# Additions of the mixing and of the residual on VectorE, the mixing bias by ScalarE inside the bank, and a new order of the steps

## The reference, cut to what matters

```python
# layer 0
Mn = conv(Wn, bn, inorm(x_c)); Mm = conv(Wm, bm, inorm(x_s))
A  = softmax(einsum('bct,bcs->bts', Mn, Mm))
x  = conv(Wo, bo, einsum('bcs,bts->bct', conv(Wl, bl, x_s), A)) + x_c
# layer 1
xa  = ln(x); sx = shift(xa) - xa
xxx = tanh((xa + sx * maa_x) @ maa_w1).reshape(b, l, 5, 32)
xxx = einsum('blfd,fde->blfe', xxx, maa_w2)            # low rank, five mixes
xk, xw, xv, xr, xg = xa + sx * (maa_stack + xxx)       # the five mixed inputs
w = exp(-exp(time_decay + tanh(xw @ td_w1) @ td_w2))
r, k, v, g = xr @ Wr.T, xk @ Wk.T, xv @ Wv.T, silu(xg @ Wg.T)
s = k_t v_t^T + w_t * s                                # scan over 128 tokens
out_t = r_t (u * k_t v_t^T + s)
x1 = x + (groupnorm(out) * g) @ Wo.T
y  = x1 + sigmoid(xr2 @ Wfr.T) * (square(relu(xk2 @ Wfk.T)) @ Wfv.T)
```

## Time and profile before

| | |
|---|---|
| median of three executions | 1966.55 us |
| the profiled execution | 1968.96 us |
| its span, first to last instruction | 1967.2 us |
| TensorE (PE) busy | 1824.0 us, 93% |
| VectorE (DVE) busy | 1843.6 us, 94% |
| ScalarE (ACT) busy | 1037.8 us, 53% |
| GpSimd (POOL) busy | 1064.5 us, 54% |
| mean granted TensorE clock | 0.978 |

### The profile page before, as it was taken

The page is one execution under the profiler, slowest core; times in us unless marked ns, Lnnn a source line. Parts: engine busy times, 40 slices in busy tenths (PEclk is TensorE's granted clock), DMA queues, the critical chain, the costliest instruction groups (busy, mean ns, idle before and its releaser), DMA issues.

```text
span 1967.2 us, 34835 instructions
## 1 busy us (share of the span) xinstructions
PE 1824.0 (93%) x12548; PEld 1276.5 (65%) x12548; DVE 1843.6 (94%) x2564; ACT 1037.8 (53%) x2177; POOL 1064.5 (54%) x822
## 2 busy tenths in 40 slices
PE   5779999999999999999999999999999999999865
PEld 3556666676666767666677666666766666676633
DVE  3599999999999999999999999999999999999981
ACT  3434556555555655554565555565555556555322
POOL 1245565556656555565555556655565565555531
PEclk8899999999999999999999999999999999999877
DMA  5233333333333333333333333333333233333320
GB/s 231 76 98 90 81 100 103 98 104 97 96 84 101 98 105 101 94 95 86 98 98 109 96 98 84 95 103 98 103 102 97 81 101 102 99 93 86 91 67 11
DMA packets 86201, 189.31 MB, mean 96 GB/s; under 512 B 18800, under 2 KB 35312, under 8 KB 85008
## 3 DMA queue, kind: packets, MB, share of 16 engines
q1 hardware_dynamic: 64528, 170.32, 31.4%
q10 hardware_dynamic: 21504, 16.78, 2.8%
HBM read 161.91 MB, written 16.78 MB: 91 GB/s over the span
## 4 chain that ended last, share of the span: by engine, by line
PE 58%; DVE 17%; POOL 15%; issue 9%; ACT 1%; POOLq 0%; DMA 0%; DVEq 0%; SPq 0%; ACTq 0%
PE bank L957 24%; POOL hrs L400 8%; PE bank L1004 6%; PE bank L964 5%; PE bank L1080 5%; DVE S L605 5%; PE bank L969 5%; DVE xf L570 3%; DVE S L614 3%; DVE S L596 2%; POOL xf L428 2%; POOL rku L434 2%; POOL S L444 2%; PE bank L1036 2%; PE bank L975 2%
## 5 line engine op out<-in xcount | busy, mean ns | idle before, releaser
L605 DVE TENSOR_TENSOR_SCAN S<-wrep,S 128x1024 f32<-128x1024 f32 x256 | 592.3, 2314 | 1.6 <-POOL S L444 1.1
L444 POOL COPY S<-s 128x8 f32<-128x8 f32 x256 | 173.4, 692 | 484.0 <-PE bank L1080 473.1
L428 POOL TENSOR_TENSOR xf<-xf,xa 128x512 f32<-128x512 f32 x160 | 337.4, 2116 | 124.1 <-DVE xf L570 124.1
L614 DVE TENSOR_TENSOR S<-S,rT 128x1024 f32<-128x1024 f32 x256 | 339.4, 1326 | 0.2
L596 DVE TENSOR_TENSOR S<-vrep,kT 128x1016 f32<-128x1016 f32 x256 | 319.1, 1247 | 3.5 <-PE bank L1080 3.4
L398 POOL TENSOR_SCALAR rstd<-mv 128x1 f32<-128x1 f32 (+1 forms) x96 | 128.6, 1340 | 236.8 <-DVE mv L510 143.6
L570 DVE SCALAR_TENSOR_TENSOR xf<-bank,par,sx 128x128 f32<-128x128 f32 x640 | 178.8, 341 | 13.3 <-PE bank L1036 9.5
L1080 PE MATMUL bank<-S,slide 128*32 128x256 f32 x2048 | 171.4, 397 | 9.5 <-DVE S L614 9.5
L400 POOL TENSOR_TENSOR hrs<-hrs,mhalf 128x32 f32<-128x32 f32 x32 | 175.5, 5485 | 2.7
L957 PEld LDWEIGHTS bank<-xf,Wk 128*128 128x128 f32 x1024 | 118.4, 194 | 50.0 <-issue 50.0
L957 PE MATMUL bank<-xf,Wk 128*128 128x128 f32 x1024 | 123.5, 280 | 25.9 <-DVE xf L570 25.9
(11 more groups left out here) (129 smaller groups left out, 3650.7 us busy)
## 6 DMA issues: line engine op xcount, KB each, us to landing
vrep<-v_dram SPq DMA_DIRECT2D x256, 512.0 KB
xc<-x_c SPq DMA_DIRECT2D x32, 256.0 KB, 4.0
xs<-x_s SPq DMA_DIRECT2D x32, 256.0 KB, 4.9
v_dram<-vT ACTq DMA_DIRECT2D x32, 256.0 KB, 2.6
xres<-xin SPq DMA_DIRECT2D x32, 256.0 KB, 6.5
out<-rr ACTq DMA_DIRECT2D x32, 256.0 KB, 4.4
Wv<-big_w SPq DMA_DIRECT2D x1, 1024.0 KB, 7.1
Wk<-big_w SPq DMA_DIRECT2D x1, 1024.0 KB, 9.1
```

The lines of the kernel that those rows point to most:

```text
L428: po.tensor_tensor(xf[:, b, :, :], xf[:, b, :, :], xa[:, :, 1:P + 1], ALU.add).then_inc(pool_mid.sem, 1)
L444: po.tensor_copy(S[:, u % 2, :, 0], s0[:, p, k:k + UJ]).then_inc(pool_wkv.sem, 1)
L605: ve_.tensor_tensor_scan(s, wrep[:, u % C, :, :].rearrange("p j t -> p (j t)"), s, 0.0, ALU.mult, ALU.add).then_inc(dve_wkv.sem, 1)
L614: ve_.tensor_tensor(s, s, rT[:, p, u % C, :].unsqueeze(1).broadcast_to([P, UJ, P]), ALU.mult).then_inc(dve_wkv.sem, 1)
```

## The change

It has four parts.

1. `mid_mix`: ScalarE first adds `maa_stack` in the bank itself (`mid_bias`, four instructions of 128 x 128 per mix). VectorE then multiplies the bank by `sx` in one instruction of 128 x 512 and adds `xa` in a second one; GpSimd's `mid_add` is gone.
2. `fin_y`: VectorE adds `x1` itself; GpSimd's `fin_out` is gone.
3. `mid_W1`: `xx` is now the stationary operand, four products of 160 columns with tokens on the partitions. ScalarE takes tanh into a new tile `txn`, TensorE transposes it back in two pieces (`mid_Wt`), ScalarE copies these to `tx` and `txg` (`mid_txt`).
4. A new order of all lists. `mid_Tx` and `mid_xa` move from the step of `b1` to the end of that of `b0`; the projections of r and g move from `b2` to `b1`; `tail_C`, `tail_To`, `tail_o`, `tail_sq` from `b3` to `b2`; `tail_Tx2`, `tail_FK`, `fin_FR`, `fin_kr` from `b4` to `b3`. The element's last piece, `fin_FV` to `fin_store`, stays in `b4`. The rings of banks and the counts follow.

```diff
 FRONT_JOBS = [(j, int(lag)) for j, lag in (x.split(":") for x in (
-    "Rp:2 G:2 V:0 Tx:1 Mn:0 Mm:0 W1:1 Mv:1 Mw:1 S0:0 S1:0 S2:0 Mk:1 Mr:1 S3:0 Vp:1 D1:1 Kp:1 Mg:1 "
-    "T0:0 T1:0 T2:0 T3:0 D2:1 E2:1 O:0").split())]
+    "Mn:0 Mm:0 S0:0 S1:0 S2:0 W1:1 Wt:1 V:0 S3:0 Mv:1 Mw:1 Mk:1 Mr:1 Vp:1 D1:1 Kp:1 Mg:1 D2:1 "
+    "E2:1 T0:0 T1:0 T2:0 T3:0 O:0 Rp:1 G:1 Tx:0").split())]
 BACK_JOBS = [(j, int(lag)) for j, lag in (x.split(":") for x in (
-    "Tx2:4 FK:4 C:3 FR:4 FV:4 Tg:3 Wo:3").split())]
+    "FV:4 Tg:3 Wo:3 Tx2:3 FK:3 C:2 FR:3").split())]
...
-            def mid_add(n, m, p, i):
-
-                f, b = ORDER[i], i % 3
-                eng.wait_ge(dve_mid.sem, dve_mid.count(f"m{f}", n))
-                po.tensor_tensor(xf[:, b, :, :], xf[:, b, :, :], xa[:, :, 1:P + 1],
-                                 ALU.add).then_inc(pool_mid.sem, 1)
...
-            def fin_out(n, m, p):
-                eng.wait_ge(dve_fin.sem, dve_fin.count("y", n))
-                po.tensor_tensor(rr[:, :], rr[:, :], x1[:, :], ALU.add).then_inc(pool_fin.sem, 1)
...
-                eng.wait_ge(pe_mid.sem, pe_mid.count(f"M{f}", n))
+                eng.wait_ge(act_mix.sem, act_mix.count(f"b{f}", n))
                 eng.wait_ge(pe_mid.sem, pe_mid.count(last_use, n if i >= 3 else n - 1))
-                ps = bank_of(f"M{f}")
-                for c in range(C):
-                    last = ve_.scalar_tensor_tensor(xf[:, b, c, :], ps[:, c * P:(c + 1) * P],
-                                                    col("maa_stack", c, MIX.index(f)), sx[:, c, :], ALU.add, ALU.mult)
-                last.then_inc(dve_mid.sem, 1)
+                ve_.tensor_tensor(xf[:, b, :, :], by_chunk(bank_of(f"M{f}")[:, :]), sx[:, :, :],
+                                  ALU.mult).then_inc(dve_mid.sem, 1)
+                eng.wait_ge(dve_mid.sem, dve_mid.count(f"m{f}", n))
+                ve_.tensor_tensor(xf[:, b, :, :], xf[:, b, :, :], xa[:, :, 1:P + 1],
+                                  ALU.add).then_inc(dve_mid.sem, 1)
...
                 ve_.tensor_tensor(rr[:, :], bank_of("FV")[:, :], rr[:, :], ALU.mult).then_inc(dve_fin.sem, 1)
+                eng.wait_ge(dve_fin.sem, dve_fin.count("y", n))
+                ve_.tensor_tensor(rr[:, :], rr[:, :], x1[:, :], ALU.add).then_inc(dve_fin.sem, 1)
...
+            def mid_bias(n, m, p, f):
+
+                eng.wait_ge(pe_mid.sem, pe_mid.count(f"M{f}", n))
+                for c in range(C):
+                    ps = bank_of(f"M{f}")[:, c * P:(c + 1) * P]
+                    last = sc.activation(ps, ps, ACT.Identity, bias=col("maa_stack", c, MIX.index(f)))
+                last.then_inc(act_mix.sem, 1)
...
-                ps = bank_of("W1")
-                for c in range(C):
-                    pe.matmul(ps[:, 0:P], w1[:, c, 0:P], xx[:, c, :], start=(c == 0), stop=(c == C - 1))
-                for c in range(C):
-                    last = pe.matmul(ps[0:DM, P:2 * P], w1[:, c, P:P + DM], xx[:, c, :],
+                for c in range(C):
+                    last = pe.matmul(bank_of("W1")[:, 0:5 * DM], xx[:, c, :], w1[:, c, :],
                                      start=(c == 0), stop=(c == C - 1))
                 last.then_inc(pe_mid.sem, 1)
+
+            def mid_Wt(n, m, p):
+
+                eng.wait_ge(act_mid.sem, act_mid.count("tn", n))
+                eng.wait_ge(*bank_free("Wt", n))
+                pe.transpose(bank_of("Wt")[:, 0:P], txn[:, 0:P], ident[:, :])
+                pe.transpose(bank_of("Wt")[0:DM, P:2 * P], txn[:, P:P + DM], ident[:, :]).then_inc(pe_mid.sem, 1)
```

More of the change, by code:

```diff
@@ L142, in build @@
         txg = sb("txg", [DM, P])
+        txn = sb("txn", [P, 5 * DM])
         xf = sb("xf", [P, 3, C, P])
@@ L415, in mid_xa0 @@
                 v0 = held(eng, regs[0], 16 * (m + 1))
-                v1 = held(eng, regs[1], dve_mid.count("xx", n - 1))
-                v2 = held(eng, regs[2], pool_mid.count("fg", n - 1))
+                v1 = held(eng, regs[1], dve_mid.count("fg", n - 1))
                 eng.wait_ge(pool_const, CONSTS)
@@ L647, in tail_x1 @@
                 eng.wait_ge(xres_copied[p], 16 * (m + 1))
-                eng.wait_ge(pool_fin.sem, pool_fin.count("out", n - 1))
+                eng.wait_ge(dve_fin.sem, dve_fin.count("out", n - 1))
                 ve_.tensor_tensor(x1[:, :], bank_of("Wo")[:, :], xres[:, p, :], ALU.add).then_inc(dve_tail.sem, 1)
@@ L733, in step @@
+                if b2: tail_o(*b2)
                 if b1: wkv_scan(*b1, 0)
+                if b0: att_rstd1(*b0)
             run(step)
@@ L894, in fin_store @@
             def fin_store(n, m, p):
-                eng.wait_ge(pool_fin.sem, pool_fin.count("out", n))
+                eng.wait_ge(dve_fin.sem, dve_fin.count("out", n))
                 dst = out[n] if isinstance(n, int) else out[bass.ds(n, 1)].rearrange("o p f -> (o p) f")
@@ L1000, in att_O @@
             def att_O(n, m, p):
+                eng.wait_ge(act_att.sem, act_att.count("v", n))
                 eng.wait_ge(*bank_free("O", n))
```

236 lines of the change are left out of this document (118 added, 118 removed).

## The result

The changed kernel takes 2006.8 us in the median (2003.4 to 2008.5) against 1967.5 us for the kernel before on the same chip: a ratio of 1.0195, interval 1.0181 to 1.0208, 39 us slower. The prediction was 1961 us with a range of 1943 to 1990; it was wrong in sign, and the time lies outside its range.

What follows compares the result with a forecast made beforehand. VectorE, busy 297.4 of 300 us, was taken as the bound. 1968.96 us profiled, +0.3 (added work against contention), +3 (att_rstd1), -9.3 (ends) gave 1963.0; less 2.4 for the median, about 1961 us, range 1943 to 1990.

Steps and rivals of the forecast that it cites:

- Mixing +40 us: VectorE's mixes, as a product and a chained addition, take 1.29 us each, +0.25 a mix, +40 us in all.
- residual +22.7 us: VectorE's residual: the product loses its 0.11 us overlap and a 0.60 us addition follows, +22.7 us over 32 elements.
- A chained start costs 0.11 us: On VectorE a dependent instruction starts 0.03 us behind its predecessor's end, where unchained neighbours overlap by 0.08 us.
- Rival F: A chained start on VectorE costs nothing, 21 us less than the forecast: 1940 us; chance 0.02.
- Contention: 72.4 us go, 10 come back: GpSimd's large instructions hold up VectorE's by 72.4 us; most goes with the additions, 10 us stays for the rest.
- Rival C: GpSimd's product r x k meets outer1, which starts 1.07 us late in each element: +24 us, 1985 us; chance 0.12.
- The wait at `att_rstd1`, 3 us: Behind scan0, VectorE may wait some 0.5 us for GpSimd's power, 17 us in 32 elements; 3 us was taken.
- Bias covered, cost nothing: ScalarE's bias delays each mix by 1.5 us, hidden as mixes stand later; cost nothing, uncovered 0.5 us.
- Low-rank part, nothing counted, -0.4 to +0.5 us per element: TensorE's low-rank work shrinks by 0.4 us but adds a round trip through ScalarE; nothing was counted.
- TensorE fits with some tenths in hand: Between unit 5's read and the next read0, TensorE needs 16.5 to 17 us, ScalarE 0.6, against VectorE's 17.6.
- Rival B: VectorE starts to wait, att_xin for O or read0 for rT; at 0.6 us a step 1980 us; chance 0.27.
- The ends: Fill and drain: the end, from last read to variance, saves 9.3 us; the start counts 0, within 3 either way.

Runs made afterwards that it cites:

- e7_unchained: e1_rk_late with another VectorE instruction between the product and the addition of each mix and of the residual; 1966.2 us, ratio 0.9984.
- e4_old_order: The kernel before with only VectorE's additions and ScalarE's bias from the change, old order and old low-rank part; 2091.4 us, ratio 1.0627.
- e1_rk_late: The changed kernel with GpSimd's product r x k moved behind the initial columns of unit 3, as before; 1979.6 us, ratio 1.0060.
- e9_more_unchained: The kernel of e7_unchained with six more VectorE pairs drawn apart and the addition of xr behind scan 6; 1979.1 us, ratio 1.0054.
- e5_lowrank_ring: The changed kernel with the old low-rank products, keeping the transposes' slot in the ring of banks; 2026.0 us, ratio 1.0289.
- e8_start: e1_rk_late with the low-rank product W1 and the first mix taken earlier, in step 1 only; 1979.0 us, ratio 1.0055.

## Why the prediction was wrong, point by point

- **VectorE sets the pace.** Right in the middle; the step is its list plus small waits.
- **Mixing +40 us, residual +22.7 us.** Nearly right. By the table above the mixes cost 1.43 us a step, 46 in all (0.71 and 0.61 for a pair, where 1.29 was worked out), the residual 0.73, 23 in all.
- **A chained start costs 0.11 us.** Right, by the pairs of e7_unchained. Rival F falls; the rule of the Trainium skill behind it, "VectorE: DVE Perf Modes", section "The DRAIN you can't avoid", does not hold here (0.60 against 0.71 us).
- **Contention: 72.4 us go, 10 come back.** This is the step that failed: what is left of the contention was sized at 10 us and measured 31.7. That the additions were the cause is right for some 61 of the 72.4 us (e4_old_order); the other 11 were already the product r x k, which stays, so the 10 taken are about what it had cost in its old place. In the new place it costs 31.7 us by the mean of L596, near the upper end of the bounds (0 to 34). Moving it away in e1_rk_late gave 27 back, some 3 of them by the clock, while it still cost 0.14 us a step there. By the table the net gain is 1.16 us a step, where 2.26 - 0.31 = 1.95 was in the sum. Two choices stood behind the 10. The place: "comes while VectorE does read0 and outer1" was right, and both of these have two inputs in SBUF, so there was no cover at all. The row: the copy at 1076.87, where waiting GpSimd let two of VectorE's instructions pass, was taken as the likely course; but the product doesn't find read 0 running, it starts 0.09 us ahead of it, behind the small nmr, and then holds it. Rival C was this mechanism with the right price and, but for element 12, the wrong victim (read 0, not outer 1). In element 12 the product did find read 0 running, and it did not let outer 1 pass as the copy had done: it went as rival C had it. Why the copy waited for two instructions and the product for one is open. The Trainium skill, "GPSIMD Engine Reference", section "8. Key points", warned of just such pairs of instructions; it gives no price, and the price was in the trace.
- **The wait at `att_rstd1`, 3 us.** It doesn't occur in the middle steps of the changed kernel: its power starts 0.36 us before the scan does (1088.62 and 1088.98) and is 0.23 us long. The mechanism was real all the same: e9_more_unchained, where the aggregation ends at the scan, has 0.71 us of it a step, where "some 0.5" was worked out.
- **Bias covered, cost nothing.** Right in the steady state: VectorE waits for it 8.7 us in the whole run, in five places. The cover is the new order; without it the waits for bias are 66.1 us (e4_old_order), 2 us a step, where the text had 0.5.
- **Low-rank part, nothing counted, -0.4 to +0.5 us per element.** The work was sized about right (0.6 us less); that it counts for nothing was wrong: without it the new order would have been 0.8 us a step longer (e5_lowrank_ring). The kernel before had no such waits, so this is no term of the miss; it means that the new order left TensorE no room for the old part.
- **TensorE fits with some tenths in hand.** Half right. Rival B was right that `xin` waits for O, wrong on when: not in each step by 0.3 to 0.6 us, but in five steps by 1.6, each behind a fall of the clock. The prediction read the clock as full because it was full before. In the new order TensorE's waits stand together (1.07, 0.68 and 1.10 us for `Tx2`, sum 5 and M, 3.05 us a step) and it didn't stay so. 8 us.
- **The ends.** The end is right: 12.9 to 3.2 us, -9.7 against -9.3 (from step 31 on -8.3). The start is wrong: +9.3, where 0 within 3 was given. The text counted what stands ahead of P v (4.1 us, and 4.5 came: 55.8 to 60.3), but P r stands behind T and O of the next element too, and neither ScalarE's scalings, which moved behind bias g, nor the lower clock had a term. How the 8 us divide between the two wasn't tried; e8_start only rules out the order of W1 and of the first mix.

Put as a sum: 1961, and 25 (contention, 0.79 a step), 6 (mixes, 0.18 a step), 2 (residual and the rest of the step), 8 (the five late `xin`), 9 (start), less 3 (`att_rstd1`): 2008, against 2006.8 measured. Two thirds of the miss, contention and clock, were shown by experiments; the start was only read from the trace.

## What to carry to other kernels

When large GpSimd work leaves, ask of each piece that stays what VectorE is doing at the moment when it is released, and what the piece costs in its present place. If both neighbours have two SBUF inputs, price it at the worst row: the same 1.27-us product cost 1.05 or 0.14 us by its place. A tuned loop at 99% has no slack for a move of the small instructions either: place a statistics step so that GpSimd's short ones fall beside a bank read. And an engine that follows the bound closely is a second bound: its savings and its clock both arrive at the first one.
